# Attention scores on quarters of the array, the depthwise convolution partly in PSUM, attended outputs taken up two units late, and far units one a step

## The reference, cut to what matters

```
x1 = depthwise_conv3x3(x) + dw_b
ca = eca(x1)                                  # needs the mean of x1 over all pixels
q, k, v = wq x, wk x, (wv x) * ca             # 1x1 convolutions
head 0 (8 channels): windows of 8x8, 64 queries, 64 keys
head 1 (8 channels): windows of 8x8, 64 queries, 16 keys (k, v halved by a strided convolution)
y = softmax(q k / sqrt(8)) v                  # per image, window and head, windows shifted by 4
out = po_w (y + sigmoid(sa_w y) * x1) + po_b + x0
```

## Time and profile before

| | |
|---|---|
| median of 3 runs | 809.02 us (808.78 to 811.79) |
| time of the profiled execution | 807.16 us |
| its span | 804.9 us |
| busy: DVE | 624.1 us, 78% |
| busy: PE | 617.0 us, 77% (x13480) |
| busy: POOL | 559.6 us, 70% |
| busy: ACT | 529.4 us, 66% |
| mean granted PE clock | 0.942 of full |

### The profile page before, as it was taken

One profiled execution on the slowest core, in us unless ns is written; L12 is line 12 of the kernel. 1 busy time (PEld: TensorE's weight loads), 2 busy tenths in 40 slices (PEclk: granted clock), 3 DMA queues, 4 the chain that ended last, 5 costly groups with the idle time before them and its releaser, 6 DMA issues. The chain is left out here.

```text
span 804.9 us, 31946 instructions
## 1 busy us (share of the span) xinstructions
PE 617.0 (77%) x13480; PEld 471.2 (59%) x13480; DVE 624.1 (78%) x815; ACT 529.4 (66%) x838; POOL 559.6 (70%) x441
## 2 busy tenths in 40 slices
PE   5977888888599998777676777787787788777622
PEld 1325566655334664666675677777777677666522
DVE  2377999999641223779688899999999997999935
ACT  2555677776321323878677878888989877987505
POOL 3028878886141000689789799999999998999940
PEclk9997999999799999999899999999999998999967
DMA  4000000000068114887778766767767666776202
GB/s 175 1 0 1 2 0 0 0 0 0 0 150 195 21 19 105 179 192 166 155 175 182 173 176 160 209 163 199 181 181 183 176 163 158 195 199 177 69 3 104
DMA packets 40587, 92.29 MB, mean 115 GB/s; under 512 B 21263, under 2 KB 21391, under 8 KB 40208
## 3 DMA queue, kind: packets, MB, share of 16 engines
q1 hardware_dynamic: 37314, 89.57, 44.8%
q10 hardware_dynamic: 3150, 0.88, 0.5%
HBM read 79.47 MB, written 3.28 MB: 103 GB/s over the span
## 5 line engine op out<-in xcount | busy, mean ns | idle before, releaser
L1258 PE MATMUL PS<-region 64*64 64x112 f32 (+5 forms) x11136 | 386.0, 265 | 118.5 <-issue 62.6
L1258 PEld LDWEIGHTS PS<-region 64*64 64x64 f32 (+1 forms) x11136 | 316.7, 139 | 174.6 <-issue 104.4
L844 DVE TENSOR_TENSOR region<-PS,region 128x1024 f32<-128x1024 f32 (+1 forms) x256 | 298.8, 1204 | 41.4 <-PE PS L1258 35.0
L559 POOL TENSOR_TENSOR region<-region 128x960 f32<-128x960 f32 x128 | 240.1, 1876 | 32.2 <-DVE region L844 31.9
L1102 ACT ACTIVATE region<-region 128x1152 f32<-128x1152 f32 x128 | 149.2, 1165 | 36.4 <-PE PS L1258 32.0
L1099 ACT ACTIVATE region<-region,cst 128x1152 f32<-128x1152 f32 x128 | 159.4, 1245 | 7.2 <-DMA region<-px_scratch 5.9
L562 POOL TENSOR_TENSOR region<-region 128x320 f32<-128x320 f32 x128 | 117.4, 917 | 10.0
L855 DVE TENSOR_REDUCE region<-region 128x32 f32<-128x736 f32 x128 | 116.4, 910 | 2.3 <-POOL region L562 2.1
L1258 PE MATMUL PS<-wg,xp 64*64 64x144 f32 x1024 | 84.3, 292 | 6.0 <-issue 6.0
L486 POOL TENSOR_TENSOR region<-region,cst 128x1024 f32<-128x1024 f32 x32 | 61.4, 1920 | 31.4 <-PE PS L1333 25.3
L1258 PEld LDWEIGHTS PS<-wg,xp 64*64 64x64 f32 x1024 | 65.7, 137 | 14.9 <-issue 13.7
(11 more groups left out here) (139 smaller groups left out, 633.7 us busy)
## 6 DMA issues: line engine op xcount, KB each, us to landing
region<-px_scratch SPq DMA_DIRECT2D x256, 288.0 KB, 4.7
out<-region SPq DMA_DIRECT2D x4, 512.0 KB, 3.0
region<-xp SPq DMA_DIRECT2D x8, 140.2 KB, 2.9
region<-xp SPq DMA_DIRECT2D x8, 140.1 KB, 2.9
region<-xp SPq DMA_DIRECT2D x8, 140.0 KB, 2.9
cst<-in_consts SPq DMA_DIRECT2D x1, 1102.5 KB, 8.9
region<-xp SPq DMA_DIRECT2D x8, 132.0 KB, 2.8
region<-xp SPq DMA_DIRECT2D x8, 131.9 KB, 2.7
```

The source lines that it names most:

```text
L559: pool.tensor_tensor(two_rows[:, :, :, 0:NA - FOLD], two_rows[:, :, :, 0:NA - FOLD], two_rows[:, :, :, FOLD:NA], ALU.add).then_inc(half_re ...
L844: v.tensor_tensor(uu[:, 2 * u:2 * u + 2, :, lo:hi], PS[:, banks:banks + 2, 0:(hi - lo) * C].rearrange("p h (a o) -> p h o a", o=C), awf[:, ...
L1258: return nc.tensor.matmul(o, l, r, start=start, stop=stop)
```

## The change

It does seven things.

1. Scores on quarters: POOL masks keys onto 4 groups of columns instead of 8 (`ks`, `h0`, `h0k`), the upper 64 partitions (images 4 to 7) and the lower 64 are multiplied apart, in 64x64 quarters, 320 columns each (256 for head 0, 64 for head 1), into banks 0 (lower) and 1 (upper). DVE reads both banks in one instruction.
2. The values of head 1 are spread by a POOL instruction of their own (`vb`).
3. The three taps of the convolution's middle row are three PE matmuls with diagonal matrices (`dwd`, made once by POOL) that accumulate in bank 2 or 5; the other six are added by DVE in PSUM, the last of them writes SBUF. `lead` on ACT and its sum on POOL go away. The bias is added in `row_sum`, which ACT now does for all 8 blocks.
4. `normalise_heads` is one DVE instruction instead of two.
5. PE takes up attend(n-2) in step n, and it stands between the middle tap and values(n); back is of unit n-3. ACT writes unit n-3.
6. The transposed output goes into the second 128 columns of bank 7; `probs` on PE waits for the write before it.
7. `far_image_rows` and `far_taps` issue one unit a step over 7 steps; ACT takes the rows out after chunk 3, DVE's far_sums stands four steps later.

```diff
@@ gpsimd
+            for t in range(3):
+                pool.tensor_tensor(dwd[:, t, :], ident, w_("dw")[:, 3 + t:4 + t].to_broadcast([P, P]), ALU.mult).then_inc(dwd_ready, 1)
...
                     pool.tensor_tensor(
-                        kb[:, u].rearrange("p w (b k) -> p w b k", b=B),
-                        kw[...].unsqueeze(2).to_broadcast([P, 2, B, K1]),
-                        mid(c_("h0"), 2).unsqueeze(3).to_broadcast([P, 2, B, K1]), ALU.mult).then_inc(staged, 1)
+                        ks[:, u, :, 0:4 * K1].rearrange("p w (b k) -> p w b k", b=4),
+                        kw[...].unsqueeze(2).to_broadcast([P, 2, 4, K1]),
+                        mid(c_("h0"), 2).unsqueeze(3).to_broadcast([P, 2, 4, K1]), ALU.mult).then_inc(staged, 1)
...
+                        ks[:, u, :, 4 * K1:] ... [P, 2, 4, K2] ... c_("h0k")
+                        vb[:, u] ... [P, 2, B, K2] ... c_("h1")
-                rows = x13[:, bass.ds(WS * i + WS, WS), 1:W]
-                pool.tensor_tensor(rows, rows, tap1, ALU.add).then_inc(lead_ready, 1)
@@ vector
-            for hd in range(2):
-                v.tensor_tensor(on[...][:, :, CS * hd:CS * (hd + 1)], PS[:, 3, ...], end(...), ALU.mult).then_inc(on_ready, 1)
+            own = PS[:, 3, 0:2 * (P + CS)].rearrange("p (t k) -> p t k", t=2)[:, :, 0:P]
+            v.tensor_tensor(on[:, u, :].rearrange("p (b t c) -> p t b c", t=2, c=CS), own..., end(...), ALU.mult).then_inc(on_ready, 1)
...
+                    v.scalar_tensor_tensor(here if t < 5 else x13[:, bass.ds(WS * i, WS), :], src, wcol, here, ALU.mult, ALU.add).then_inc(conv_step, 1)
+            def four_steps(i, odd):
+                for jj, which in enumerate((range(0, 2), range(2, 4), range(4, 5), range(5, 6))):
...
+                        invert(n - 2, jj % 2)
...
+                        normalise_heads(n - 2, jj % 2)
...
-            v.reduce_sum(small[:, 48 + NWR:49 + NWR], x1[:, (H - WS) * W:], axis=AX.X).then_inc(eca_step, 1)
@@ scalar
-            def lead(i):
...
-                a.activation(rows, rows, ACT.Copy, accum_out=...).then_inc(x1_sum, 1)
+                a.activation(rows, rows, ACT.Identity, bias=w_("dw_b"), accum_out=...).then_inc(x1_sum, 1)
...
-                    write(n - 2, WS * i + SHIFT - (WS if jj < 2 else 0), 16 * ((jj - 2) % 4) + SHIFT)
+                    write(n - 3, WS * i + SHIFT - (WS if jj < 3 else 0), 16 * ((jj - 3) % 4) + SHIFT)
@@ tensor
             def scores(n, u):
-                pe.wait_ge(staged, done(n, 2))
+                pe.wait_ge(staged, done(n, 3))
                 pe.wait_ge(q_staged, done(n, 2))
                 pe.wait_ge(sub_ready, 2 * n + 4)
-                for w in range(2):
-                    mm(PS[64 * w:64 * (w + 1), u, :], qs[:, u, w, :], kb[:, u, w, :])
-                    ins = mm(PS[64 * w:64 * (w + 1), 2, 0:P], qs[:, u, w, :], kvb[:, u, w, 0, :])
+                for w, j in ((0, 0), (1, 1), (0, 1), (1, 0)):
+                    part = slice(64 * j, 64 * (j + 1))
+                    ins = mm(PS[64 * w:64 * (w + 1), j, 0:4 * (K1 + K2)], qs[part, u, w, :], ks[part, u, w, :])
+            def middle(i, odd, t):
+                if t == 0 and not (isinstance(i, int) and i < 2):
+                    pe.wait_ge(conv_step, 6 * (i - 1))
...
+                ins = mm(grid(PS[:, 2 if odd else 5, :], W)[:, :, ca:cb], dwd[:, 1 + dx, :],
+                         xe3[:, bass.ds(WS * i, WS), ca + dx:cb + dx], start=t == 0, stop=t == 2)
             def probs(n, u):
                 pe.wait_ge(exp_ready, done(n))
                 pe.wait_ge(pt_out, 2 * n + 4)
+                pe.wait_ge(ye_out, n if not isinstance(n, int) else max(n, 2))
+            def four(i, odd):
                 for jj in range(4):
                     n = 4 * i + jj
                     scores(n, jj % 2)
                     probs(n - 1, (jj - 1) % 2)
+                    if jj < 3 and not isinstance(i, int):
+                        middle(i + 1, not odd, jj)
+                    attend(n - 2, jj % 2)
                     values(n, jj % 2)
-                    back(n - 2, jj % 2)
-                    attend(n - 1, (jj - 1) % 2)
+                    back(n - 3, (jj - 3) % 2)
...
                 for i in range(SPC):
+                    near, then = ((s - (PAIRS - 1) * NCH - e) * SPC + i for e in (1, 4))
+                    if 0 <= near < FU:
+                        far_image_rows(near)
+                    if 0 <= then < FU:
+                        far_taps(then)
```

More of the change, by code:

```diff
@@ L684, in normalise_heads, with conv_taps @@
                 dve.wait_ge(ot_ready, free(n))
-                for hd in range(2):
[L686 to L693, removed]
+                own = PS[:, 3, 0:2 * (P + CS)].rearrange("p (t k) -> p t k", t=2)[:, :, 0:P]
+                v.tensor_tensor(on[:, u, :].rearrange("p (b t c) -> p t b c", t=2, c=CS), own.rearrange("p t (b c) -> p t b c", c=C)[:, :, :, 0:CS],
+                                end(sm[:, u, 2, :].rearrange("p (t b) -> p t b", t=2), CS), ALU.mult).then_inc(on_ready, 1)
+            def conv_taps(which, i, odd):
                 first, last = (isinstance(i, int) and i == e for e in (0, NWR - 1))
-                before = 0 if first else (KK - 2) * i
+                order = [(dy, dx) for dy in ((1, -1) if last else (-1, 1)) for dx in (-1, 1, 0)]
+                sums = grid(PS[:, 2 if odd else 5, :], W)
                 for t in which:
-                    dy, dx = taps[t]
+                    dy, dx = order[t]
                     wcol = w_("dw")[:, 3 * (dy + 1) + dx + 1:3 * (dy + 1) + dx + 2]
@@ L702, in conv_taps @@
                     src = xe3[:, bass.ds(WS * i + above + dy, WS - above - below), ca + dx:cb + dx]
-                    dst = x13[:, bass.ds(WS * i + above, WS - above - below), ca:cb]
+                    here = sums[:, above:WS - below, ca:cb]
                     if t == 0:
-                        ins = v.tensor_scalar(dst, src, wcol, w_("dw_b"), ALU.mult, ALU.add)
+                        dve.wait_ge(middle_ready, i + 1)
                     else:
[L707 to L711, removed]
@@ L1355, in back @@
             def back(n, u):
-                pe.wait_ge(on_ready, done(n, 2))
+                pe.wait_ge(on_ready, done(n))
                 pe.wait_ge(ye_out, n + 2)
-                nc.tensor.transpose(PS[:, 5, 0:P], on[:, u, :], ident).then_inc(ot_ready, 1)
+                pe.wait_ge(pt_out, done(n + 2, 2) if not isinstance(n, int) or n < 30 else done(31, 2))
+                nc.tensor.transpose(PS[:, 7, P:2 * P], on[:, u, :], ident).then_inc(ot_ready, 1)
+            pe.wait_ge(dwd_ready, 3)
+            for t in range(3):
+                middle(0, False, t)
             for n in range(4):
```

181 lines of the change are left out of this document (91 added, 90 removed).

## The result

| | before | after |
|---|---|---|
| median of the runs on one chip | 808.9 us (4 runs) | 843.79 us (4 runs, 839.37 to 857.77) |
| profiled execution | 807.16 us | 840.2 us |
| its span | 804.9 us | 838.4 us |
| mean granted PE clock | 0.942 | 0.941 |
| start of the gate after attention (DVE, before L740, after L736) | 209.93 us | 249.52 us |

The ratio is 1.0446, with a 95% interval of 1.0385 to 1.0506: slower, as forecast (832 us, range 815 to 849), by 12 us more than forecast. The whole loss lies in attention: its end comes 39.6 us later, and from the first product to the end of the span the kernel before takes 481.4 us and the changed one 474.9.

A forecast was written before the change was run, and what follows sets the result against it. DVE was taken to bound attention before the change. The new ring and attention's ends gave +25.3 us, the far units -2.2: +23.1 on 807.16 is 830.3, plus 1.9 for the runs' median, so 832 us, range 815 to 849.

The forecast's parts named there:

- DVE loses its place as the bound: Attention: DVE, busy 17.66 of 17.80 us a block before, would work about 13 of 21.6.
- The ring: Attention: each unit's round through PE and ACT sets the pace, 21.59 us a block against 17.76; chance 0.72.
- The ring's size: Attention: sum of the round's parts on PE and ACT, 5.46 us a unit with a tap, 4.60 without.
- The 0.61 us of `row_sum`: Attention, ACT: added once a block, in the step behind a row_sum.
- The clock: Rival: PE's granted clock falls in attention through idle pieces over 0.5 us; +22 us, 854 us, chance 0.07.
- Scores four at a time: Attention, PE: quarters run together, 0.55 to 0.65 us against 1.23; rival, not in parallel, 841 or 869 us, chance 0.11.
- The cover of 0.2 us: Attention: scores(n+1) would end ahead of exps, write and hand-over, with no more than 0.2 us to spare.
- The sign that PE would wait some 0.5 us: Attention, changed profile: PE would wait about 0.5 us for the write or exps before probs.
- First and last units: Attention's ends: probs 3 at its old time within 1 us, last block +2.3 us, tail 0.
- The last block: Attention's end, without middle taps: 18.5 us against 16.17, so +2.3.
- the tail: Attention's end: attend(30) behind probs(31) against DVE's dropped sum; 0 us, bounds -0.7 and +1.5.
- Far units: Deformable steps: one unit a step fits PE's slack and saves POOL's wait; -2.2 us, bounds 0 and -5.5.

The follow-up runs named there:

- run 9: Run 6 with row_sum moved on ACT from ahead of write to behind it; 783.72 us, ratio 0.9768 to the kernel before.
- run 2: The changed kernel with ACT's stage, exps and row_sum put ahead of its copies of values; 793.18 us, against 806.13 for the kernel before.
- run 5: The changed kernel with PE's values ahead of middle tap and attend, and four buffers instead of two for v0 and v1; 786.89 us.
- run 6: The changed kernel with its part 5 undone (attend of unit n-1, back and write of n-2); 791.73 us, ratio 0.9774 to the kernel before.
- run 1: The changed kernel with PE's values(n) moved ahead of the middle tap and attend(n-2); 841.37 us.
- run 10: Run 6 with the four quarter matmuls of scores in plain order; 784.63 us.
- run 8: The kernel before with only the far units changed (one a step, rows out after chunk 3, sums four steps later); 803.86 us, ratio 1.0008.
- run 3: The changed kernel with row_sum moved on ACT from behind exps to ahead of values; 830.82 us.
- run 4: The changed kernel with one middle tap on PE instead of three, the convolution lacking the other two; 849.9 us.
- run 7: Run 6 with ACT's stage, exps and row_sum ahead of values, as in run 2; 789.77 us, ratio 0.9763 to the kernel before.

## Why the prediction was right, and where it fell short

**DVE loses its place as the bound: right.** 13.07 and 13.10 us of a block against 13 forecast; taps 739 ns in the mean of 32 (groups by line of the changed kernel, 80 to 232 us):

```profile
L710 DVE SCALAR_TENSOR_TENSOR PS<-region,wr,PS 128x504 f32<-128x504 f32 (+2 forms) x32 | 23.7, 739 | 0.0
```

0.70 was taken, 0.75 was the nearer row. Beside POOL's work they don't grow. In run 9 two taps run wholly beside POOL's multiplies:

```profile
113.63 0.74 DVE L710 SCALAR_TENSOR_TENSOR PS<-region,wr,PS 128x504 f32<-128x504 f32 x1
...
117.64 0.75 DVE L710 SCALAR_TENSOR_TENSOR PS<-region,wr,PS 128x512 f32<-128x512 f32 x1
```

```profile
112.89 1.05 POOL L489 TENSOR_TENSOR region<-region,cst 128x512 f32<-128x512 f32 x1 [1.86 <-PE PS L1329]
...
116.91 1.05 POOL L489 TENSOR_TENSOR region<-region,cst 128x512 f32<-128x512 f32 x1 [2.02 <-PE PS L1329]
```

With all operands in SBUF a tap beside POOL took up to 1.98 us. The Trainium skill (SBUF — State Buffer, the section on port contention) says that a DVE instruction with at most one SBUF input keeps clear of GpSimd outside DVE's two-port modes, and these rows agree.

**The ring sets the pace: right, and shown** by runs 2, 5 and 6, which shorten or open it each in another place and give blocks of 17.11, 16.27 and 16.17 us with the same work. Its second closing through the v0/v1 buffers is not in the prediction; it did not change the sum, but without it run 1 could not be read.

**The ring's size: four terms too small.** The tap took 0.95 us (0.86 forecast, from 512 columns in two passes), attend 1.21 (1.16), the transposes of values 0.65 to their last end (0.59), the hand-over from PE to ACT 0.12 (132.85 to 132.97; 0.03 forecast). That makes 5.74 and 4.80 where 5.46 and 4.60 stood. The tap's term came from starts among equals, and attend's from a difference of two stretches in which 64-column weights follow each other; here the shapes change (a full-array tap, then 64-column attend, then transposes). The hand-over came from a single pair of rows. The 0.61 us of `row_sum` came in its own step, not in the one behind it. A block so is 22.50 us at full clock where 21.59 stood, and six like the first would have given +28.4 us (135.0 against 106.55) instead of +23.0.

**The clock: the part that failed.** The prediction set the fall aside as a rival of its own, at 0.07, with a price for it as a quarter of all units. In the sum it put the clock's cost at nothing. What happened is between: one step in four is slow, from the second block on, the one behind `row_sum`. The five blocks take 120.2 us (105.35 to 225.57) where five of the first would take 112.5: +7.7 us. Forecast and rival both held in part, and they add. The argument against it, a clock of 1.00 with idle pieces of 0.18 and 0.49 us, was of pieces much shorter than those the ring leaves: 1.43 to 1.51 us before scores in each step and, in the `row_sum` step, 0.63 more before probs. The prediction had itself worked out idle pieces of more than 0.5 us, longer than any that the row covered, and still gave the rival 0.07.

**Scores four at a time: right, but slower than hoped.** 0.70 us from start to probs (134.48 to 135.18), against 0.55 to 0.65. The cover of 0.2 us shrank to nothing: write ended at 135.03, probs could start at 135.18 by either. No price was paid, and none was left. The sign that PE would wait some 0.5 us for the write or exps before probs did not show, except in the `row_sum` step: PE's pause lies in front of scores, not behind them, and by the trace scores(n+1) close the ring in the other steps as much as the write does.

**First and last units.** Probs 3 came at 82.85, as said, but by luck. From probs 0 to probs 3 the changed kernel took 17.00 us (65.85 to 82.85) against 14.29 (68.52 to 82.81): the loss had begun, with a granted clock of 0.50 from 68 to 72 us (the kernel before had 0.50 from 60 to 70). Probs 0 came 2.67 us earlier, and its start differs as much between executions of nearly the same code (68.05 in run 6, 63.34 in run 10). The last block took 19.27 us (225.57 to 244.84) against 18.5, by the same terms; the tail 0.3 us more than before, against 0. Attention so comes to 36.2 + 3.1 + 0.3 = 39.6 us against 25.3 forecast: 5.4 of the 14.3 are the ring's terms, 7.7 the clock, 0.8 the last block, 0.3 the tail.

**Far units: open.** -2.2 us was forecast, and the stretch from first product to the end is 6.5 us shorter. But it is no measure of them: run 2 (481.7 us) and run 6 (481.5) have the same far part, and run 8 has it alone at 480.6, all like the kernel before (481.4). Run 10, with the instructions of run 6 in these steps, took 476.4: the stretch differs by 5 us from one execution to another. The wait did go, as run 8 shows, and the whole did not move by more than its interval of 0.4% either way. POOL's 2.22 us, which the forecast took for the gain, were not had: most of what the shorter wait gave was taken up by other waits of DVE (run 8).

So the 9.9 us between 840.2, the profiled execution, and 830.3 are +14.3 in attention, -3.9 behind it (588.9 us to the end of the span against 595.0, which is -6.1 where -2.2 was forecast) and -0.5 around the span.

**What was luck.** The number fell into the range although attention lost 39.6 us where 25.3 stood. The stretch behind it came out 3.9 us better than forecast, for no reason that a run shows, and the early start of probs 0 hid another 2.7. Without both the time would have been near 849, the upper end of the range.

**What stays open.** What exactly makes the clock fall: it fell behind the `row_sum` step, but not in the first block; in run 3 it fell in the first block and in none after; in run 1 the step behind `row_sum` took some 7.15 us in the third to fifth block but 5.53 in the sixth, with the same pause; and it fell more in run 4, whose PE works less. No run held all else fixed and varied the pause alone. The quarters or the convolution in PSUM were not tried one by one on the old order.

## What to carry to other kernels

Before an operation is moved within an in-order engine, write down the ring through all engines that one unit goes round and add it up from rows; if it is longer than the busiest engine's work, the move costs the difference, however much work the rest of the change saves. Look for each ring's second closing, above all a pair of buffers that the delayed reader holds a step longer. A later take-up needs more buffers (four for two in run 5) and a place behind what the other engine waits for; with both (run 5), or with the take-up left where it was (run 6), the same work was 2% faster than the kernel before. Where the engine that waits has work that needs nothing of the ring, putting that first helped where that engine did wait (run 2), and not where it didn't (run 7).

## What the runs showed of the hardware

- **PE's clock fell after a pause, and with less work for PE it fell more.** The granted clock was 1.00 in the step with `row_sum` and 0.76 in the 7.21 us behind it; over six blocks it was 0.82 with two of three taps taken out (run 4) and 0.94 with them. The slow step of the next block begins at 0.54:

```profile
141.50:143.50 2.00, 1.98 (x7) 1.32 (x7) 1.23 (x4) 0.77 (x2) 0.00 (x0) 0.54 0.00 0
```

  That is near the 1.2 GHz level, and its five transposes took 1.17 us where they take 0.77 at full clock:

```profile
141.52 1.17 PE L1338 MATMUL PS<-cst,region 128*128 128x128 f32 x5 [0.63 <-ACT region L1016]
```

- **Quarters of 64x64 ran four at a time at 320 columns** in either order: 0.70 us for eight instructions, where full-height matmuls of the same unit needed 1.23. By the 0.86 us for 512 columns a single float32 matmul of 320 columns would take some 0.54 us and four one after another 2.15 (estimates).
- **A float32 tap of 504 or 512 columns from full-array weights** took 0.94 to 0.95 us to the next load when attend's 64-column weights followed, against 0.86 between equals. Another shape alone does not bring it: in run 6, where a 128x128 transpose follows, it was 0.86 (113.16 to 114.02).
